# Score groups ahead of the transposes beside them, and the first six quads' reciprocal totals moved by ScalarE's queue

## The reference, cut to what matters

```python
q, k, v = proj(x, Wk, bk), proj(ctx, Wk, bk), proj(ctx, Wv, bv)
scores = q @ k^T / sqrt(32)                       # causal mask
a      = softmax(scores) ; dist = sqrt((total - cumsum(a)) * |i - j|)
scores = scores * clip(exp(-softplus(gamma) * dist), 1e-5, 1e5)
out    = softmax(scores) @ v                      # second softmax
x1 = layer_norm(x + out @ Wo^T + bo)
x2 = layer_norm(x1 + relu(x1 @ W1^T + b1) @ W2^T + b2)
```

## Time and profile before

| | |
|---|---|
| runs | 1519.01, 1512.74, 1510.36 us; median 1512.74 |
| the profiled execution | 1510.36 us, its span 1508.6 us (1.8 us lie around it) |
| TensorE (PE) busy | 1444.4 us, 96% |
| VectorE (DVE) busy | 1082.1 us, 72% |
| ScalarE (ACT) busy | 1026.3 us, 68% |
| GpSimd (POOL) busy | 164.8 us, 11% |
| chain that ended last | PE 87%, DMA 4%, DVE 4%, ACT 2% |
| granted TensorE clock, mean | 0.987 |

### The profile page before, as it was taken

How to read it: one execution, slowest core, us unless ns; L and a number is a source line. 1 busy time by engine, 2 the same in 40 slices (tenths; PEclk the granted TensorE clock), 3 DMA queues, 4 the chain that set the end, 5 groups by cost and what they waited for, 6 DMA issues and landing times.

```text
span 1508.6 us, 34270 instructions
## 1 busy us (share of the span) xinstructions
PE 1444.4 (96%) x12896; PEld 1207.0 (80%) x12896; DVE 1082.1 (72%) x3780; ACT 1026.3 (68%) x2626; POOL 164.8 (11%) x192
## 2 busy tenths in 40 slices
PE   5687899999999999999999999999999999999997
PEld 5465788888888888888888888888888888888886
DVE  6796868777787768677677867767776776867533
ACT  4574777777776777677676867768777676776622
POOL 4213210101001010100101001010000101010100
PEclk9898999999999999999999999999999999999999
DMA  7755656667676656565666566666665666665976
GB/s 280 279 202 206 242 211 251 230 239 245 223 258 220 241 194 238 206 215 214 218 243 216 217 206 215 218 212 243 210 233 197 228 228 210 221 212 188 330 284 252
DMA packets 76260, 346.01 MB, mean 229 GB/s; under 512 B 17600, under 2 KB 18624, under 8 KB 43456
## 3 DMA queue, kind: packets, MB, share of 16 engines
q1 hardware_dynamic: 64256, 335.06, 62.3%
q0 software_dynamic: 11264, 8.76, 1.9%
q10 hardware_dynamic: 576, 0.00, 0.0%
HBM read 316.16 MB, written 27.53 MB: 228 GB/s over the span
## 4 chain that ended last, share of the span: by engine, by line
PE 87%; DMA 4%; DVE 4%; ACT 2%; issue 1%; POOL 1%; SPq 1%; DVEq 0%; ACTq 0%; POOLq 0%
PE bank L226 24%; PE bank L228 22%; PE bank L227 22%; PE bank L486 9%; PE bank L500 6%; PE bank L520 2%; PE bank L537 1%; DMA w_ring<-w_split 1%; DVE w_sb L1298 1%; DMA w_split<-w_ring 1%; DMA ring_raw<-w 1%; DVE w_sb L1310 1%; DMA zi_row<-zi_out 1%; ACT w_sb L884 1%; PE bank L523 1%
## 5 line engine op out<-in xcount | busy, mean ns | idle before, releaser
L226 PE MATMUL bank<-xt_hi,w_ring 128*128 128x256 f32 x1024 | 298.8, 292 | 4.5 <-DMA w_ring<-w_split 2.3
L227 PE MATMUL bank<-xt_lo,w_ring 128*128 128x256 f32 x1024 | 290.5, 284 | 0.0
L228 PE MATMUL bank<-xt_hi,w_ring 128*128 128x256 f32 x1024 | 290.5, 284 | 0.0
L1286 DVE CUSTOM_DVE_ANT_0 s_sb<-bank,mask 128x256 f32<-128x256 f32 (+7 forms) x512 | 130.4, 303 | 215.4 <-PE bank L486 214.0
L914 ACT COPY pt_sb<-bank 128x512 f32<-128x512 f32 x192 | 111.6, 581 | 172.1 <-PE bank L500 172.1
L226 PE MATMUL bank<-w_ring,h_hi 128*128 128x512 f32 x512 | 207.1, 404 | 0.5 <-DMA w_ring<-w_split 0.5
L904 ACT ACTIVATE p_sb<-w_sb,nm 128x32 f32<-128x32 f32 (+7 forms) x512 | 205.4, 404 | 3.1 <-DVE nm L1325 3.1
L226 PEld LDWEIGHTS bank<-xt_hi,w_ring 128*128 128x128 f32 x1024 | 196.8, 192 | 11.9 <-issue 11.0
L884 ACT ACTIVATE w_sb<-s_sb,nm 128x161 f32<-128x161 f32 (+7 forms) x512 | 164.1, 404 | 55.6 <-DVE nm L1294 55.6
L228 PE MATMUL bank<-w_ring,h_lo 128*128 128x512 f32 x512 | 201.1, 393 | 0.0
L227 PE MATMUL bank<-w_ring,h_hi 128*128 128x512 f32 x512 | 200.5, 392 | 0.0
(11 more groups left out here) (127 smaller groups left out, 2956.8 us busy)
## 6 DMA issues: line engine op xcount, KB each, us to landing
w_ring<-w_split SPq DMA_DIRECT2D x252, 1024.0 KB, 5.1
w_split<-w_ring SPq DMA_DIRECT2D x32, 512.0 KB, 5.1
x_raw<-x_t SPq DMA_DIRECT2D x16, 512.0 KB, 3.7
c_raw<-ctx_t SPq DMA_DIRECT2D x16, 512.0 KB, 4.8
u_sb<-x_rows SPq DMA_DIRECT2D x16, 512.0 KB, 6.0
ring_raw<-w SPq DMA_DIRECT2D x32, 256.0 KB, 5.3
zi_row<-zi_out POOLq DMA_DIRECT2D x64, 128.0 KB, 5.2
out<-rows SPq DMA_DIRECT2D x15, 512.0 KB, 9.9
```

Of the source, the lines that this page charges most:

```text
L226: nc.tensor.matmul(dst, a_hi, b_hi, start=start, stop=False)
L227: nc.tensor.matmul(dst, a_hi, b_lo, start=False, stop=False)
L228: return nc.tensor.matmul(dst, a_lo, b_hi, start=False, stop=stop)
L1286: m = nc.vector.tensor_tensor_reduce(out=s_sb[:, c % 2, W_AT[b] + 1:W_AT[b] + 1 + WIDTH[b]], in0=s_bank[n % 2][:, at:at + WIDTH[b]], in1=m ...
```

## The change

TensorE's list in `step`: each score group that followed a group of transposes now stands ahead of it. ScalarE's list in `first()`: it issues the store and the load of the reciprocal totals of the quads (0, 0) to (1, 1), on semaphores of their own; GpSimd moves the others as before.

```diff
             def step(i, now, last, ffn, done, ahead):        # TensorE
...
                     hidden(i - 2, 2)
+                if now:
+                    scores(i, 0, 1)
                 if last:
                     transposes(i - 1, 2, 1)
-                if now:
-                    scores(i, 0, 1)
                 if ffn:
                     add_hidden(i - 2, 1)
+                if now:
+                    scores(i, 0, 2)
                 if last:
                     transposes(i - 1, 2, 2)
                 if now:
-                    scores(i, 0, 2)
...
                     hidden(i - 2, 4)
+                if now:
+                    scores(i, 1, 1)
                 if last:
                     transposes(i - 1, 3, 1)
-                if now:
-                    scores(i, 1, 1)
                 if ffn:
                     add_hidden(i - 2, 3)
+                if now:
+                    scores(i, 1, 2)
                 if last:
                     transposes(i - 1, 3, 2)
                 if now:
-                    scores(i, 1, 2)
...
                 if now:
+                    scores(i, 2, 1)
                     transposes(i, 0, 1)
-                    scores(i, 2, 1)
...
                 if now:
+                    scores(i, 2, 2)
                     transposes(i, 0, 2)
-                    scores(i, 2, 2)
...
                 if now:
                     attend(i, 0)
+                if now:
+                    scores(i, 3, 0)
                 if last:
                     turn_rows(i - 1, 0)
-                if now:
-                    scores(i, 3, 0)
+                if now:
                     transposes(i, 1, 0)
...
                 if last:
                     turn_rows(i - 1, 1)
                 if now:
+                    scores(i, 3, 2)
                     transposes(i, 1, 1)
-                    scores(i, 3, 2)
...
+            def zi_store(i, c):                               # ScalarE
+                act.wait_ge(zi2_ok, NQ * i + c + 1)
+                act.dma_start(zi_out[c], z2[:, c]).then_inc(zi_act_st, 16)
+
+            def zi_load(i, c):
+                act.wait_ge(zi_act_st, 16 * (NQ * i + c + 1))
+                if c >= 2 or i > 0:
+                    act.wait_ge(cc_ok, NQ * i + c - 1)
+                act.dma_start(zi_row[:, c % 2], zi_load_from(i, c)).then_inc(zi_act_in[c % 2], 16)
...
             def first():                                      # ScalarE
...
                 effect(0, 2)
                 turned(0, 1, 0)
+                zi_store(0, 1)
                 ahead_copy(0, 1)
                 concat_high(0, 0)
                 first_exp(0, 3)
+                zi_load(0, 1)
                 turned(0, 1, 1)
...
                 features(0, 0)
                 effect(1, 2)
                 turned(1, 1, 0)
+                zi_store(1, 1)
                 concat_high(1, 0)
                 features(0, 1)
                 first_exp(1, 3)
+                zi_load(1, 1)
                 turned(1, 1, 1)
...
             def first():                                      # GpSimd
...
                 for n in range(2 * NQ):
-                    if n >= 2:
-                        totals_out((n - 2) // NQ, (n - 2) % NQ)
                     if n == 2:
                         inputs_high(1)
```

More of the change, by code:

```diff
@@ L179, in build @@
         zi2_ok = sem("zi2_ok")
-        zi_st = sem("zi_st")
-        zi_in = [sem(f"zi_in{n}") for n in range(2)]
+        zi_st, zi_act_st = sem("zi_st"), sem("zi_act_st")
+        zi_in, zi_act_in = ([sem(f"{n}{m}") for m in range(2)] for n in ("zi_in", "zi_act_in"))
         cc_ok = sem("cc_ok")
@@ L228, in three_passes, with zi_load_from @@
             return nc.tensor.matmul(dst, a_lo, b_hi, start=False, stop=stop)
+        ZI_ACT = NQ + 2
+        def zi_load_from(i, c):
+            return zi_out[c].rearrange("(h r) b -> h (r b)", h=HQ).unsqueeze(1).broadcast_to([HQ, R, R * NB])
         def over_batches(first, step, final):
@@ L1004, in first @@
                 turned(0, 0, 0)
+                zi_store(0, 0)
                 first_exp(0, 2)
+                zi_load(0, 0)
                 turned(0, 0, 1)
@@ L1026, in first @@
                 turned(0, 2, 0)
+                zi_store(0, 2)
                 ahead_copy(1, 1)
@@ L1029, in first @@
                 first_exp(1, 0)
+                zi_load(0, 2)
                 turned(0, 2, 1)
@@ L1038, in first @@
                 turned(0, 3, 0)
+                zi_store(0, 3)
                 ahead_copy(2, 1)
@@ L1041, in first @@
                 first_exp(1, 1)
+                zi_load(0, 3)
                 turned(0, 3, 1)
@@ L1052, in first @@
                 turned(1, 0, 0)
+                zi_store(1, 0)
                 first_exp(1, 2)
+                zi_load(1, 0)
                 ahead_copy(3, 1)
@@ L1332, in concat @@
                 dve.wait_ge(av_mm, NQ * i + c + 1)
-                dve.wait_ge(zi_in[c % 2], 16 * ((NQ * i + c) // 2 + 1))
+                n = NQ * i + c
+                if n < ZI_ACT:
+                    dve.wait_ge(zi_act_in[c % 2], 16 * (n // 2 + 1))
+                else:
+                    dve.wait_ge(zi_in[c % 2], 16 * ((n - ZI_ACT) // 2 + 1))
                 nc.vector.tensor_tensor(cc_sb[:, c % 2].rearrange("p (b r) -> p b r", r=R),
@@ L1683, in _, with totals_out @@
             nc.gpsimd.tensor_scalar(nb2_col[:], b2_col[:], -1.0, None, ALU.mult).then_inc(const_ok, 1)
-            def zi_store(i, c):
-                pool.wait_ge(zi2_ok, NQ * i + c + 1)
+            def totals_out(i, c):
+                n = NQ * i + c
+                pool.wait_ge(zi2_ok, n + 1)
                 pool.dma_start(zi_out[c], z2[:, c]).then_inc(zi_st, 16)
[L1689 to L1698, removed]
+                pool.wait_ge(zi_st, 16 * (n - ZI_ACT + 1))
+                pool.wait_ge(cc_ok, n - 1)
+                pool.dma_start(zi_row[:, c % 2], zi_load_from(i, c)).then_inc(zi_in[c % 2], 16)
             def add_bias(i):
```

## The result

The changed kernel takes 1497.95 us, median of four runs (1493.6 to 1499.14), against 1515.21 us for the kernel before, in runs of the same session. The ratio is 0.9892, with a 95% interval of 0.9864 to 0.9919: 1.1% faster. The profiled execution took 1497.32 us with a span of 1495.5 us; the one before took 1510.36 with 1508.6. So the two profiles differ by 13.1 us where the medians differ by 17.3. What follows accounts for the 13.1.

The account below looks back on a forecast made before the run. TensorE was taken to bound the steps, a chain over several engines, twice through GpSimd, `first()`. The new order's 9.5 us plus the moved DMAs' 10.8 (6.8 + 4.5 - 0.5) made 20.3 us off: 1491 us, range 1484 to 1502.

Parts of the forecast that it names:

- A, seven pairs: In each step, scores ahead of transposes at seven places: 0.05 us each, 0.35 us a step.
- A, eighth place: In each step, scores ahead of the turned rows, covering a 0.23 us wait: 2.52 us for 2.85, 0.33 less.
- A, the sum: TensorE's new order over 14 steps: 14 x (0.35 + 0.33) = 9.5 us, between 3.2 and 11.8.
- I cost this at nothing: In the steps, transposes and their `turned` some 0.8 us later: no cost, as the slack before `attend` is 3.1 us.
- B, first wait: In `first()`, quad (0, 0): `concat` no longer waits for GpSimd's totals; 6.8 us, between 3.3 and 9.0.
- B, second wait: In `first()`, quad (0, 3): `concat` loses its 4.46 us wait; 3.5 to 5.1 us, taken as 4.5.
- B, costs: In `first()`, the last load, of quad (1, 1), delays a `turned` TensorE needs: 0.5 us, between 0 and 3.
- Rival 1: Another bound in `first()` takes back the DMA move's gain, leaving perhaps 2 us of it: 1501 us; chance 0.10.
- rival 2: In the steps, the swap is worth only the covered wait, by count of mode changes, 4.6 us: 1497; chance 0.07.
- rival 3: In the steps, later transposes make TensorE wait, 22 us come back: 1514 us, no change; chance 0.06.
- Rival 4: In `first()`, ScalarE's queue stands at six loads for their stores to land, 28.5 us: 1527 us, slower; chance 0.03.

Follow-up runs that it names:

- pairs alone: Kernel before with only the seven score/transpose pairs swapped, eighth place and totals' DMAs as before: 1514.14 us, one run; steps 83.44 / 89.04 us.
- experiment 3: Kernel before with totals' DMAs on ScalarE's queue for two quads only, 1504.99 us (one run), against the one with all six, 1506.01 us.
- B alone: Changed kernel with TensorE's old order in the steps, so only the six quads' DMAs moved to ScalarE's queue: 1506.01 us, ratio to before 0.9938.
- experiment 4: Changed kernel with totals of (15, 3) ahead of concat of (15, 2): 1494.2 us; or with the last two quads' totals on ScalarE's queue: 1499.71 us.

## Why the prediction was right

1491 us was forecast, 1497.95 measured: within the range, with the sign and the mechanisms of both parts right, and a gain of 17.3 us in the medians, 13.1 in the two profiles, for 20.3. Both parts came out a little smaller than forecast, and one term, the end, was missing.

- **A, seven pairs.** Right. The interval went from 1.767 to 1.722 us at six swapped places, and the seventh, without a row of its own, from 3.247 to 3.202: 0.045 each, for 0.05 forecast. The pairs alone gave 0.31 us a step, which is 7 x 0.045. The Trainium skill, TensorEngine Tiling (Array Packing), section Key Properties, says that changing the tiling mode drains TensorE. If each change cost the same the pairs would be worth nothing, and with that the trace does not agree: 0.31 us came without one change less. What a single change costs no run here shows. The 0.42 of my upper bound for the pairs has no row behind it either.
- **A, eighth place.** Forecast 0.33, measured 0.42 in the starts: my value was too high for the turned rows, which hold TensorE for 0.49 us (656.41 to 656.90) instead of 0.53, and for the transposes behind them, 0.36 instead of 0.41.
- **A, the sum.** 9.5 us forecast, 7.9 measured. The step that failed is "I cost this at nothing": I checked the slack of the `turned` before `attend`, and it held, no wait for `pt_sb` appears in the `step`s. I did not read the slack of the next `queries_keys`, which starts earlier because everything ahead of it on TensorE is shorter, while VectorE's `x_lo` follows only in part. By that product the swaps have taken 0.69 us out of TensorE's list. The slack gave 0.29 of it, and `x_lo`, which follows the earlier scores, ends 0.23 us earlier in the step; the other 0.17 us came back as a wait. Work that gets shorter also moves the use of everything that comes from other engines.
- **B, first wait.** 6.8 forecast; TensorE went on 6.2 us earlier (71.30 for 77.48) and the next scores 6.2 us earlier (81.5 for 87.75). The times were near: store at 46.64 for 47, `concat` at 67.09 for 66 to 67, no wait. The load came at 49.81, sooner than the 53 I took. But only 3.62 of the 6.8 us was the wait for the totals. Another 3.39 was the instruction held under GpSimd's casts, and my sum took it away without a reason. It went because GpSimd, rid of the totals, cast the next inputs 5.2 us earlier (61.39 for 66.60), ahead of that instruction: right, but not worked out. The clock did not stay up after the shorter wait: 0.83 granted between 73 and 83 us instead of 0.50, with 3.4 us of half clock in place of 10.2; most of what that gave, an estimated 1.0 us (half of the 5.4 and 3.4 us that TensorE worked at half clock, 2.7 less 1.7), went into a wait of 0.63 us for `x_lo`.
- **B, second wait.** 4.1 us came here for 4.5, 10.3 us of lead at 119.04 where I had 6.8 + 4.5 = 11.3. The two kernels of experiment 3 give 4.0. The clock did not stay up: the 24 scores still took 1.50 us.
- **B, costs.** The 0.5 us for the last load was not there: the wait ahead of the transposes behind it is 1.31 us in both kernels. But 1.2 us of the lead were lost again, most of it by a longer stretch of half clock after 153.15, which I had not priced. Taken together the stage gives 9.07 us for 10.8.
- **The end.** Not in the forecast at all: 2.51 us of TensorE's wait and 1.4 of the clock behind. I had read what A makes late inside a `step`, and nothing of `final()`, where A acts too: TensorE has none of the work there that hides VectorE in the `step`s, and a landing has to be early for both concats. Over all executions with A and the old order of `final` the rest is 2 to 10 us longer than without A, so this one was the mildest. So part A by itself is worth less than its 7.9 us in the steps as long as the line in `final` is not moved.
- **The rivals.** Rival 1 (the first stage gives perhaps 2 us) is refuted by 9.1 us for B alone, rival 2 by the steps with the seven pairs alone, rival 3 by the absence of any wait for `pt_sb` in them. Rival 4 needed landings over 5.6 us on ScalarE's queue in `first()`; the six stores took 1.4 to 4.3 (median 3.9). Its mechanism is real all the same: with the DMAs alone one store took 5.8 us and cost TensorE 1.1, and at the end of the program, in experiment 4, one of 6.5 us held ScalarE for 5.6.

## What to carry to other kernels

Where an engine's in-order list holds a small, urgent DMA behind work that waits for something else, give it to the queue that is idle at that time: 15 us of standing became 0.23. When the bound engine gets faster, list every hand-over into it and subtract the gain from each slack, those in the prologue and the last stage too, and read slacks under a microsecond in the starts, since the list of waits does not hold them. In VectorE's last stage put what starts a transfer ahead of what waits for one: one moved line was worth 2 to 7 us by the rests of the profiles (192.6 to 195.2 against 188.2 and 190.2). And a load that waits for its own store belongs on an idle queue alone: on one that is in the chain a late landing can hold the work behind it, as it did here twice (1.1 and 2.2 us of TensorE's time).

## What the hardware showed that I had not expected

**ScalarE's queue issues a DMA while ScalarE still computes.** The load at 69.58 us lies in the middle of the eight exponentials of `first_exp`, which run from 68.14 to 70.69, although it stands behind them in the list. It starts when its store has landed: that was issued at 65.31 and took 4.25 us. That is why the load of (0, 0) came 3 us earlier than I took. An issue held the queue for 0.32 us for a store and 0.53 for a load in the median, with 0.56 and 0.71 for the same two on GpSimd's. In the changed kernel, tile `zi_out` up to 170 us (line, engine, count: min/median/max ns, from and to us):

```profile
L927 ACTq DMA_DIRECT2D zi_out<-z x6: 320/321/357, 46.6 to 152.8; - x6
...
L933 ACTq DMA_DIRECT2D zi_row<-zi_out x6: 531/534/1103, 49.8 to 160.8; - x6
```

By the Trainium skill, DMA: Bandwidth & Descriptors, section Issuing engines are not separate DMA queues, initiating DMAs on several engines saves only the time of initiating. What ScalarE's shorter issue saved, 0.24 and 0.18 us, is the smallest part of what the move brought here; the greater part is the 14.8 us for which the store had stood behind other waits in GpSimd's list.

**The order of two small groups between two large blocks has a price.** Twenty-four scores on 32 by 32 tiles and four transposes on the whole array take 0.045 us less when the scores come first, whichever of the two blocks stands ahead.

**Landings near the end are slower with the new order, and I can't say why.** From issue to landing the loads of the last two quads took 7.9 to 10.7 us in the six profiles with A and the old order of `final`, 6.5 to 8.9 in the three with the moved line, and 4.6 to 8.1 in the four without A. GpSimd's queue alone is not the cause, by experiment 4. That A moves these loads against the megabyte loads of weights beside them was not tried by itself.

**While TensorE has work, the half clock follows a wait of it in every case seen**, for 3.4 to 10.2 us, and not the same for the same wait: after the wait for weights near the end it fell in the changed kernel (2.04 us) and not before the change (2.30 us). Spreads of 2.7 us between executions of one kernel at the first `step` (166.81 to 169.50) come with that.
